# Transposing the last rows by DMA and using the taps' halves for one channel only, in a long convolution on one core

## What is computed

```python
W = weights[condition]                      # one 128 x 128 matrix of 16 per batch entry
x = x + einsum('bct,bcd->bdt', x, W)
K = 2.0 * einsum('hn,hnl->hl', Ct, exp(dtA[:, :, None] * arange(L))).real
y = irfft(rfft(x, 2L) * rfft(K, 2L))[..., :L] + x * D[:, None]   # causal convolution per channel
x = x + y * (arange(L)[None, :] < length[:, None])[:, None, :]
```

## Time and profile before

| | us |
|---|---|
| median of 3 runs | 1081.11 |
| lowest, highest | 1080.15, 1083.68 |
| the profiled execution | 1082.12 |
| its span, first to last instruction | 1080.3 |

### The profile page before, as it was taken

The page is one execution under the profiler, slowest core; times in us unless marked ns, Lnnn a source line. Parts: engine busy times, 40 slices in busy tenths (PEclk is TensorE's granted clock), DMA queues, the critical chain, the costliest instruction groups (busy, mean ns, idle before and its releaser), DMA issues.

```text
span 1080.3 us, 29253 instructions
## 1 busy us (share of the span) xinstructions
PE 1004.6 (93%) x11632; PEld 739.8 (68%) x11632; DVE 772.3 (71%) x1711; ACT 548.5 (51%) x1166; POOL 502.7 (47%) x545
## 2 busy tenths in 40 slices
PE   8977788777899999999999999999999999999998
PEld 5322234233347888888888788888888888888886
DVE  4989940000017888888888888888888888888885
ACT  2634334244444556556456555555555555555553
POOL 2200042101205556656666665665665665665530
PEclk9999999999999999999999999999999999999999
DMA  8999999999989999999999999999999999999994
GB/s 343 423 423 423 424 422 422 377 424 424 423 326 294 284 271 262 228 227 224 217 239 233 214 238 224 225 234 228 222 232 226 234 221 229 225 225 232 208 223 118
DMA packets 169543, 304.96 MB, mean 282 GB/s; under 512 B 78194, under 2 KB 111346, under 8 KB 161218
## 3 DMA queue, kind: packets, MB, share of 16 engines
q1 hardware_dynamic: 169090, 302.64, 98.4%
q10 hardware_dynamic: 160, 0.26, 0.1%
q0 software_dynamic: 160, 0.20, 0.1%
HBM read 152.37 MB, written 134.41 MB: 265 GB/s over the span
## 4 chain that ended last, share of the span: by engine, by line
PE 74%; DMA 18%; ACT 3%; DVE 2%; issue 2%; SPq 1%; ACTq 0%
DMA u_scratch<-stage 17%; PE bank L590 16%; PE bank L599 15%; PE bank L555 13%; PE bank L541 10%; PE bank L529 7%; PE bank L567 7%; PE bank L596 5%; ACT stage L708 2%; DVE x_t L1001 1%; PE bank L608 1%; DMA x_f<-in_x 1%; DVE st_sb L991 0%; ACT ring L708 0%; DVE u_t L986 0%
## 5 line engine op out<-in xcount | busy, mean ns | idle before, releaser
L590 PE MATMUL bank<-toep,u_t 128*128 128x192 f16 (+1 forms) x3072 | 342.7, 220 | 2.0 <-issue 1.8
L599 PE MATMUL bank<-g_sb,st_sb 128*128 128x256 f16 x1536 | 305.9, 273 | 0.5 <-issue 0.4
L529 PE MATMUL bank<-x_f,w_buf 128*128 128x512 f32 x512 | 237.3, 608 | 57.2 <-ACT stage L708 35.5
L541 PE MATMUL bank<-ident,u_row 128*128 128x128 f32 x1024 | 277.4, 274 | 0.2
L730 ACT ACTIVATE st_sb<-bank 128x128 f16<-128x128 f32 x448 | 123.8, 276 | 289.6 <-PE bank L567 198.0
L590 PEld LDWEIGHTS bank<-toep,u_t 128*128 128x128 f16 x3072 | 231.3, 98 | 16.3 <-issue 2.4
L529 PEld LDWEIGHTS bank<-x_f,w_buf 128*128 128x128 f32 x512 | 93.4, 192 | 192.4 <-issue 109.8
L1016 DVE COPY_PREDICATED o_sb<-mask,u_row 128x512 f32<-128x512 uint8 x256 | 205.8, 804 | 16.6 <-issue 16.5
L986 DVE SCALAR_TENSOR_TENSOR u_t<-bank,u_t 128x512 f16<-128x512 f32 x256 | 176.2, 689 | 37.4 <-ACT u_t L722 35.4
L596 PE MATMUL bank<-toep,x_t 128*128 128x64 f16 x2048 | 188.3, 193 | 1.9 <-issue 1.9
L431 POOL TENSOR_TENSOR lam_sb<-eyes,lam_v 128x512 f16<-128x512 f16 x64 | 75.2, 1176 | 235.7 <-PE bank L567 235.7
(11 more groups left out here) (135 smaller groups left out, 912.6 us busy)
## 6 DMA issues: line engine op xcount, KB each, us to landing
x_f<-in_x SPq DMA_DIRECT2D x64, 1024.0 KB, 19.6
u_row<-u_scratch SPq DMA_DIRECT2D x128, 512.0 KB, 5.7
out<-o_sb SPq DMA_DIRECT2D x254, 256.0 KB, 3.8
u_scratch<-stage SPq DMA_DIRECT2D x50, 1024.0 KB, 17.8
toep<-k_scratch SPq DMA_DIRECT2D x64, 256.0 KB, 6.0
u_scratch<-ring SPq DMA_DIRECT2D x13, 512.0 KB, 14.7
u_scratch<-kept SPq DMA_DIRECT2D x10, 448.0 KB, 7.0
gt_sb<-g_sb SPq DMA_TRANSPOSE x124, 5.4
```

What stands on the lines that cost most here:

```text
L529: last = pe.matmul(bank[:, 4 * (n % 2) + k, :], w_buf[n % XS][:, :], x_f[n % XS][:, k * 512:(k + 1) * 512], start=True, stop=True)
L541: last = pe.transpose(bank[:, 4 + q, g * P:(g + 1) * P], u_row[c % 4][:, h, g, tb * P:(tb + 1) * P], ident[:, :])
L590: pe.matmul(bank[:, y, col + tb * P + NM:col + Q], u[:, h, tb, a, rows_], t[:, h, b, NM:Q - tb * P], start=first, stop=False, skip_group_c ...
L599: last = pe.matmul(bank[:, y, col:col + Q], st[:, h, a, gr * ROWS:(gr + 1) * ROWS], g[:, h, b, :], start=False, stop=(m == 2), skip_group_ ...
```

## The change

For pairs c >= TURNED = 3 the last group (NG-1) of both channels (h < TH = 2) is no longer transposed on TensorE. ScalarE (`parts_hi`) and VectorE (`parts_lo`) split it, untransposed, from u_row to a new tile parts (128 x 1024 f16), and SyncE (`transpose_parts`) sends it by one DMA transpose to its place in u_t. TensorE's inputs_to_state(c) and VectorE's first x_t copy wait for that DMA (s_pt). `u_hi` and `u_lo` then move 384 columns, not 512. The corner trick with x_t stays for channel TRI = 1 alone; channel 0 multiplies the full width, 256 and 128 columns. The fold of the taps, now of channel 1 only, moves from VectorE to ScalarE. On both engines some steps change places.

```diff
@@ -39,6 +39,9 @@
 WAVES = 5
+TURNED = 3
+TH = 2
+TRI = 1
 XS = 6
@@ -89,6 +92,8 @@
         eyes = sb("eyes", [P, 2, NM], F16)
+
+        parts = sb("parts", [P, TH, 2, 2, P], F16)
         swap = sb("swap", [P, 2, NM], F16)
@@ -239,6 +245,10 @@
             return ap(t, part * NG * ROWS + at(j), [[2 * NG * ROWS, 2], [1, NB]])
+
+        def groups(c, h):
+
+            return NG - 1 if c >= TURNED and h < TH else NG
 
@@ -318,6 +328,13 @@
 
+            def transpose_parts(c):
+                sp.wait_ge(s_pl, c - TURNED + 1)
+                wait(sp, s_out, 4 * (c - 3))
+                sp.dma_start(ap(u_t[c % 4], (NG - 1) * ROWS, [[NG * ROWS, TH * 4], [1, ROWS]]),
+                             parts[:, :, :, :, :].rearrange("p h b a t -> p (h b a t)"), transpose=True)\
+                    .then_inc(s_pt, 16)
+
             def store_out(i, c, h):
@@ -374,6 +391,8 @@
                         store_half(n, 1, EARLY, H, s_kept)
+                if TURNED <= c + 1 < PAIRS:
+                    transpose_parts(c + 1)
                 if has(i, c - 1):
@@ -533,6 +552,8 @@
                 q, g, n = k // NG, k % NG, UN * i + c
+                if g >= groups(c, q // 2):
+                    return
                 if k % 8 == 0:
@@ -540,7 +561,7 @@
                                     u_row[c % 4][:, h, g, tb * P:(tb + 1) * P], ident[:, :])
-                if g == NG - 1:
+                if g == groups(c, h) - 1:
                     last.then_inc(s_ut, 1)
@@ -549,6 +570,7 @@
                 pe.wait_ge(s_ul, 4 * n + 4)
+                wait(pe, s_pt, 16 * (n - TURNED + 1))
                 wait(pe, s_stl, 7 * n)
@@ -583,16 +605,16 @@
                     pe.wait_ge(s_stl, 7 * n + NG + gr)
-                first = True
+                first, lo = True, NM if h == TRI else 0
                 for tb in range(2):
                     for a in range(2):
                         for b in range(2 - a):
-                            pe.matmul(bank[:, y, col + tb * P + NM:col + Q], u[:, h, tb, a, rows_],
-                                      t[:, h, b, NM:Q - tb * P], start=first, stop=False, skip_group_check=True)
+                            pe.matmul(bank[:, y, col + tb * P + lo:col + Q], u[:, h, tb, a, rows_],
+                                      t[:, h, b, lo:Q - tb * P], start=first, stop=False, skip_group_check=True)
                             if first:
                                 between(2 * k)
                             first = False
-                    for b in range(2):
+                    for b in range(2 if h == TRI else 0):
                         pe.matmul(bank[:, y, col + tb * P:col + tb * P + NM], x_t[c % 2][:, h, tb, rows_],
@@ -719,8 +741,25 @@
                     wait(act, s_out, 4 * (n - 3))
-                act.activation(u_t[c % 4][:, q // 2, q % 2, 0, :], bank[:, 4 + q, :], ACT.Copy, scale=US)\
+                cols = groups(c, q // 2) * ROWS
+                act.activation(u_t[c % 4][:, q // 2, q % 2, 0, 0:cols], bank[:, 4 + q, 0:cols], ACT.Copy, scale=US)\
                     .then_inc(s_uh, 1)
+
+            def parts_hi(c):
+
+                for h in range(TH):
+                    act.wait_ge(s_row[c % 4][h], 16 * (c // 4 + 1))
+                wait(act, s_pt, 16 * (c - TURNED))
+                act.activation(parts[:, :, :, 0, :],
+                               u_row[c % 4][:, 0:TH, NG - 1, :].rearrange("p h (b t) -> p h b t", t=P),
+                               ACT.Copy, scale=US).then_inc(s_ph, 1)
+
+            def fold_toeplitz(i, c):
+
+
+                act.wait_ge(s_t[c % 4], 16 * (i + c // 4 + 1))
+                act.activation(toep[c % 4][0:NM, TRI, :, 0:NM], toep[c % 4][NM:P, TRI, :, 0:NM], ACT.Copy)\
+                    .then_inc(s_tz, 1)
 
@@ -996,17 +1047,10 @@
                     dve.wait_ge(s_ul, 4 * n + 4)
+                    wait(dve, s_pt, 16 * (n - TURNED + 1))
                     wait(dve, s_out, 4 * (n - 1))
                 to = slice(NM, P) if part == 0 else slice(0, NM)
-                dve.tensor_copy(x_t[c % 2][to, :, :, :].rearrange("p h b r -> p (h b) r"),
-                                u_t[c % 4][NM:P, :, :, part, :].rearrange("p h b r -> p (h b) r")).then_inc(s_xt, 1)
-
-            def fold_toeplitz(i, c):
-
-
-                dve.wait_ge(s_t[c % 4], 16 * (i + c // 4 + 1))
-                dve.tensor_copy(toep[c % 4][0:NM, :, :, 0:NM].rearrange("p h a t -> p (h a) t"),
-                                toep[c % 4][NM:P, :, :, 0:NM].rearrange("p h a t -> p (h a) t")).then_inc(s_tz, 1)
+                dve.tensor_copy(x_t[c % 2][to, TRI, :, :], u_t[c % 4][NM:P, TRI, :, part, :]).then_inc(s_xt, 1)
 
@@ -983,8 +1027,15 @@
                 t = u_t[c % 4]
-                dve.scalar_tensor_tensor(out=t[:, q // 2, q % 2, 1, :], in0=bank[:, 4 + q, :], scalar=US,
-                                         in1=t[:, q // 2, q % 2, 0, :], op0=MUL, op1=SUB).then_inc(s_ul, 1)
+                cols = groups(c, q // 2) * ROWS
+                dve.scalar_tensor_tensor(out=t[:, q // 2, q % 2, 1, 0:cols], in0=bank[:, 4 + q, 0:cols], scalar=US,
+                                         in1=t[:, q // 2, q % 2, 0, 0:cols], op0=MUL, op1=SUB).then_inc(s_ul, 1)
+
+            def parts_lo(c):
+                dve.wait_ge(s_ph, c - TURNED + 1)
+                dve.scalar_tensor_tensor(out=parts[:, :, :, 1, :],
+                                         in0=u_row[c % 4][:, 0:TH, NG - 1, :].rearrange("p h (b t) -> p h b t", t=P),
+                                         scalar=US, in1=parts[:, :, :, 0, :], op0=MUL, op1=SUB).then_inc(s_pl, 1)
 
```

More of the change, by code:

```diff
@@ L196, in build @@
         s_st, s_sth, s_stl = (sem(n) for n in ("s_st", "s_sth", "s_stl"))
+        s_ph, s_pl, s_pt = (sem(n) for n in ("s_ph", "s_pl", "s_pt"))
         s_xt, s_tz = sem("s_xt"), sem("s_tz")
@@ L742, in _ @@
                 u_hi(0, 0, q)
-            first = (("u", 0, 3), ("g", 2, 0), ("s", 0, 1), ("s", 0, 2), ("s", 0, 3), ("u", 1, 0), ("s", 0, 4),
+            first = (("u", 0, 3), ("t", 0, 0), ("g", 2, 0), ("s", 0, 1), ("s", 0, 2), ("s", 0, 3), ("u", 1, 0), ("s", 0, 4),
                      ("s", 0, 5), ("u", 1, 1), ("s", 0, 6), ("u", 1, 2))
@@ L762, in slot @@
                             u_hi(i, of, k)
+                        elif what == "p":
+                            if of >= TURNED:
+                                parts_hi(of)
                         elif what == "o":
                             out_evac(i, of, k)
+                        elif what == "t":
+                            fold_toeplitz(i, of)
                         else:
@@ L1022, in _ @@
                 u_lo(0, 0, q)
[L1024 removed]
+            first = (("u", 0, 3), ("x", 0, 0), ("x", 0, 1), ("s", 0, 1), ("s", 0, 2), ("s", 0, 3),
                      ("u", 1, 0), ("s", 0, 4), ("s", 0, 5), ("u", 1, 1), ("s", 0, 6), ("u", 1, 2))
             def slot(i, c):
[L1028 to L1029 removed]
+                steps = (("s", c - 1, 7), ("u", c, 3), ("o", c - 2, 3), ("x", c, 0), ("x", c, 1), ("p", c + 1, 0),
+                         ("s", c, 1), ("u", c + 1, 0), ("s", c, 2), ("o", c - 1, 0), ("s", c, 3),
                          ("u", c + 1, 1), ("s", c, 4), ("o", c - 1, 1), ("s", c, 5), ("u", c + 1, 2), ("s", c, 6), ("o", c - 1, 2))
@@ L1034, in slot @@
                             state_lo(i, of, k)
-                        elif what == "t":
-                            fold_toeplitz(i, of)
                         elif what == "u":
                             u_lo(i, of, k)
+                        elif what == "p":
+                            if of >= TURNED:
+                                parts_lo(of)
                         elif what == "x":
```

5 lines of the change are left out of this document (1 added, 4 removed).

## The result

The changed kernel takes 1122.5 us (median of 4 runs, 1119.4 to 1124.8), the kernel before 1082.4 beside it (4 runs, 1080.2 to 1084.5). The ratio is 1.037, 95% interval 1.033 to 1.040: slower by 3.7%. The forecast was 1074.3 us with a range up to 1094, so it is wrong in sign and the time lies outside the range.

What follows compares the result with a forecast made beforehand. TensorE's stream of matmuls was taken as the bound, VectorE's and ScalarE's state chain close behind. Terms -26.1 +10.2 +6.1 -3 +3 +3 = -6.8 gave 1074.3 us against the median 1081.1; range 1063 to 1094.

Steps and rivals of the forecast that it cites:

- x (two halves) and parts_lo need 1.5 to 2, so nobody waits: VectorE's steps ahead of the first state_lo: 1.5 to 2 us, hidden behind TensorE's inputs_to_state of 2.27 us.
- For all this I take -3 us: Lighter VectorE, hidden ScalarE additions and u_hi freed earlier: -3 us, of small stalls worth 16 us at most.
- Waits of `advance` for state_lo of many us: Sign that the forecast is wrong: TensorE's advance waiting many us for VectorE's state_lo.
- the second: Rival: the state chain stays at 1.17 us in five steps, so blocks 3, 5, 7 gain nothing; 1083 us, chance 0.18.
- all other mishaps: Remaining share of the forecast's chances, for other mishaps that cost time: 0.03.
- The term of the DMA transpose: TensorE's inputs_to_state waiting for the transposed rows, perhaps 0.05 us a pair: +3 us, bounds 0 and +25.
- The first rival: Late rows: the transfer lands 3.5 us after toep rather than 1.8, inputs_to_state waits; +18, 1092 us, chance 0.23.
- The TensorE terms: Four transposes fewer a pair, -26.1 us; first channel without its triangle trick, wider matmuls, +10.2 us (-9 to +30).
- the state chain's floor: Blocks with an advance can't get shorter than 1.11 us; waits in blocks 3, 5, 7 cost +6.1 us (0 to +15).
- the fourth rival: A 128-wide matmul costs as much as a 192-wide one, 0.08 us: +20, 1094 us, chance 0.03.
- A quiet pair: Sign that the forecast is right: inputs_to_state 11.2 us apart in quiet pairs, 11.42 in the kernel before.
- The early slots: Slots 2 to 5, where two 448 KB stores stand ahead of the new transpose: +3 us, bounds 0 and +8.

Runs made afterwards that it cites:

- the good order with the transfer behind toep: The good order with only the new DMA transpose put back behind load_toeplitz in SyncE's list: 1105.4 us, ratio 1.017 to the kernel before.
- the good order: Changed kernel with VectorE and ScalarE steps reordered, transpose issued ahead of u_row and toep, TensorE waiting for x_t only at the second channel: 1078.4 us, ratio 0.999.
- The fastest version: The good order with TURNED = 8, so pairs 3 to 7 are transposed on TensorE: 1073.0 us, ratio 0.993 to the kernel before.
- the idle transfer: Kernel before plus a 128 x 1024 DMA transpose that no engine reads, behind toep in SyncE's list: 1106.7 us, ratio 1.025.

## Why the prediction was wrong

**The step that failed first** is the one on VectorE: "x (two halves) and parts_lo need 1.5 to 2, so nobody waits", and with it "For all this I take -3 us". Durations were taken as if VectorE were alone; they need 3.12 us where they were put. The overlay's move behind state 2, shown in the order of instructions, got no price at all. It is the larger part, 0.64 of the 0.98 us of the pair shown. The order alone in the old kernel costs 51 us. "Waits of `advance` for state_lo of many us" stood in the list of what would show it wrong, and that is what came. No rival priced it: the second has the state chain at 1.17 a step, where one step here takes 1.84, and all other mishaps had 0.03. The range ended 28 us below the time.

**The term of the DMA transpose**, +3 with 0 to +25, asked only when the rows land. They land 6.0 us after their issue at the median, sooner than the working had it (731.25 and 1.5 to 2 more is 7.0 to 7.5 us after an issue at 725.8), and TensorE waits 4.8 us for them. The issue takes 1.27 us at the median, not 2.5 to 2.9. What was missed, and is the second step that failed, is the price for everyone else. As a transfer that nobody needs it costs 25 us at that place, and there the unnamed waits, for code, are 16.1 us of TensorE's time. In the changed kernel the unnamed waits are 4.6 us only; they are 13 to 15 once VectorE's part is mended. That VectorE's delays hide them until then is likely, not shown. The first rival, late rows at +18 us, comes close in size with its 19.8 us of waits in the good order with the transfer behind toep, but as a second loss beside the first; its 1092 us would have been near by luck.

**The right steps.** The TensorE terms hold: a transpose 0.11 in the chain, advances 1.12 apart where 1.11 was given as the state chain's floor, 1.22 for an even block of the first channel (1.21 forecast). Two 256-wide matmuls of 0.11 and three 128-wide ones take 0.39, so 0.057 for 128 columns where 0.055 was taken, and the fourth rival falls. A quiet pair of 11.29 us against 11.2 is found once the order is mended. The early slots were sized at +3 (0 to +8): taking the transfer out of pairs 3 to 7 gives 5.4 us, though TensorE then makes 20 transposes more, 2.1 us by their 0.107, so they cost some 7.5 in the good order (an estimate). The fastest version lies at 1073.0, near the forecast's 1074.3. That is in part luck: it has another order and five more pairs without the transfer, and the sum had counted neither. It shows that the TensorE side of the sum can be had, not that the sum was right.

**What stays open** is how the transfer behind toep makes TensorE's code late. The unnamed waits are 13 to 16 us in four kernels with the transfer at that place, but 4.6 in the changed kernel itself. Where it is moved or absent they are 0 to 4.8, with 6.9 in the kernel that has the changed order without the transfer, and with the waits for x_t taken out in the one that has the triangle for both channels. Those of 16.1 us are also less than the 25 us lost. In the good order with the transfer put back ScalarE's parts_hi also waits for the previous transfer, since there is one parts tile, and u_hi stands behind it; the idle transfer shows that this is not needed for the loss.
